# Index loads of two tiles each, fewer waits on TensorE and ScalarE, and four store buffers, in the edge loops of a graph network on one Trainium2 core

## The reference, cut to what matters

```
for s in range(S):                      # S = 2
    ce = concatenate([e, n[senders], n[receivers]], axis=-1)
    e = e + _ln(_mlp(ce, edge_blk_w0[s], ...), ...)
    agg = segment_sum(e, receivers, num_segments=num_nodes)
    cn = concatenate([n, agg], axis=-1)
    n = n + _ln(_mlp(cn, node_blk_w0[s], ...), ...)
```

## Time and profile before

| what | us |
|---|---|
| median of 3 runs (23509.02 to 23590.83) | 23560.08 |
| profiled execution, its own time | 23779.25 |
| its span, first to last instruction | 23777.4 |
| busy: PE / PEld / DVE / ACT / POOL | 12398.6 / 9600.5 / 7767.6 / 2986.5 / 12971.1 |
| mean granted TensorE clock | 0.627 |

### The profile page before, as it was taken

The page is one execution under the profiler, slowest core; times in us unless marked ns, Lnnn a source line. Parts: engine busy times, 40 slices in busy tenths (PEclk is TensorE's granted clock), DMA queues, the critical chain, the costliest instruction groups (busy, mean ns, idle before and its releaser), DMA issues. The chain is left out here.

```text
span 23777.4 us, 256036 instructions
## 1 busy us (share of the span) xinstructions
PE 12398.6 (52%) x61970; PEld 9600.5 (40%) x61970; DVE 7767.6 (33%) x22504; ACT 2986.5 (13%) x5247; POOL 12971.1 (55%) x13518
## 2 busy tenths in 40 slices
PE   0555565554232322325555656655556666666665
PEld 0444444443222222223444444444434444544454
DVE  2333333333111111112334434333333344343342
ACT  0222222221000000001111111111111111111111
POOL 2556565655666666662555555455435555555552
PEclk9566555565555555555667666666666666666675
DMA  1122222221000000001333333333323333333330
GB/s 50 52 54 56 54 55 55 55 55 47 12 11 11 11 11 11 11 11 22 99 102 107 107 102 104 103 105 104 103 60 94 100 98 99 99 99 98 99 101 14
DMA packets 2031268, 1570.78 MB, mean 66 GB/s; under 512 B 1340117, under 2 KB 1497177, under 8 KB 2029449
## 3 DMA queue, kind: packets, MB, share of 16 engines
q10 hardware_dynamic: 932082, 898.84, 11.7%
q0 software_dynamic: 446304, 295.04, 8.6%
q1 hardware_dynamic: 652511, 373.44, 5.7%
HBM read 961.50 MB, written 604.22 MB: 66 GB/s over the span
## 5 line engine op out<-in xcount | busy, mean ns | idle before, releaser
L720 POOL DMA_INDIRECT s_gt<-ta_d,s_ix x6448 | 6187.6, 960 | 5660.7 <-DMA s_ix<-in_src_s 2441.5
L863 PE MATMUL psw<-g_R,g_P 128*128 128x80 f32 (+1 forms) x12896 | 2673.2, 372 | 4261.8 <-ACT g_sg L793 3414.1
L863 PEld LDWEIGHTS psw<-g_R,g_P 128*128 128x128 f32 x12896 | 2568.8, 305 | 4795.9 <-issue 3827.8
L720 POOL DMA_INDIRECT g_gt<-xs_d,g_ix x3224 | 3048.8, 946 | 2077.7 <-DVE g_R L749 1106.8
L720 POOL DMA_INDIRECT g_gt<-ys_d,g_ix x3224 | 3049.7, 946 | 1798.9 <-issue 990.0
L608 DVE TENSOR_TENSOR g_P<-ps,dlT 128x1024 f32<-128x1024 f32 x806 | 985.3, 1222 | 5610.4 <-remote 4927.6
L863 PEld LDWEIGHTS psw<-s_R,s_P 128*128 128x128 f32 x12896 | 1908.9, 222 | 1705.1 <-issue 1702.8
L863 PE MATMUL psw<-s_R,s_P 128*128 128x64 f32 x12896 | 1877.4, 298 | 1057.3 <-issue 1020.0
L831 PE MATMUL ps<-e_w,s_hT 128*128 128x128 f32 x6448 | 1342.6, 375 | 1956.5 <-ACT s_hT L788 1679.1
L848 PE MATMUL ps<-s_Pt,s_Bw 128*64 128x128 f32 x12896 | 1535.7, 370 | 1009.8 <-issue 1008.2
L831 PEld LDWEIGHTS ps<-e_w,s_hT 128*128 128x128 f32 x6448 | 1181.8, 274 | 2084.2 <-ACT s_hT L788 1346.1
(11 more groups left out here) (289 smaller groups left out, 12961.8 us busy)
## 6 DMA issues: line engine op xcount, KB each, us to landing
s_dl<-dl_d SPq DMA_DIRECT2D x404, 512.0 KB
seg_d<-s_sg ACTq DMA_DIRECT2D x806, 256.0 KB
seg_d<-g_sg ACTq DMA_DIRECT2D x403, 320.0 KB
z_d<-g_rT ACTq DMA_DIRECT2D x403, 256.0 KB
s_z<-z_d ACTq DMA_DIRECT2D x403, 256.0 KB, 3.0
s_Bw<-tb_d ACTq DMA_DIRECT2D x3224, 32.0 KB
s_Bw<-tb_d SPq DMA_DIRECT2D x3224, 32.0 KB
s_gt<-ta_d,s_ix POOLq DMA_INDIRECT x6448
```

What stands on the lines that cost most here:

```text
L720: eng.indirect_dma_start(out=gt[k][:, s, :], out_offset=None, in_=table[:, :], in_offset=bass.IndirectOffsetOnAxis(ap=ix[h][:, r * G + s:r ...
L863: last = eng.matmul(psw[:, SP_ * t:SP_ * t + FS], P[k][:, s, :], R[k][:, s, :], start=True, stop=True)
```

## The change

It does five things, all in `edge_loop`.

1. `ix` gets four buffers of two tiles instead of two buffers of four. SP loads the indices of tiles j+2 and j+3 at every even j. In place of the four waits on landed gathers there is one, for `used` of tile j-5: `p_pre` in s0 and s1, `v_msg` in g1 and g2. At even j this also takes the place of the wait (for `p_pre` of tile j-6) ahead of SP's windows. In the program text the load now stands behind that of `dl` and, in g1, behind that of `z`.
2. `sg` and `rT` get four buffers; their writers wait for the store of four tiles ago.
3. PE loses waits: on the previous layer norm and silu, on landed gathers, windows and `z` (in s0, s1), on `v_p`. Those on landed data move to DVE, ahead of `Pt` of the same tile. In g1 PE waits for ACT's `zr` once, ahead of the segment sum instead of ahead of the transposes.
4. ACT loses its waits on `v_ln`, on `p_x`, and those ahead of its windows, and in s1 ahead of `z`.
5. In g1 and s0 DVE waits for `p_rt` ahead of `P` in place of `p_seg` there and `p_rt` ahead of `R`.

```
-s_ix, s_g, s_z, s_so, s_ro, s_dl ... (("ix", 2), ("g", 8), ("z", 8), ("so", 2), ("ro", 2), ("dl", 2))
+s_ix, s_g, s_z, s_so, s_ro, s_dl ... (("ix", 4), ("g", 8), ("z", 8), ("so", 4), ("ro", 4), ("dl", 2))
-ix = many("ix", [128, 4 * G], I32)
+ix = many("ix", [128, 2 * G], I32, n=4)
-sg = many("sg", [128, G * FS])
+sg = many("sg", [128, G * FS], n=4)
+used = p_pre if expand else v_msg
-    rT = many("rT", [128, 512])
+    rT = many("rT", [128, 512], n=4)
 def windows(eng, which, j, b, first):
-    done(eng, p_pre, j, L_BW + 4)
-    settle(eng, s_m[0])
...
 # SP
-def indices(q, i, b):
-    h = ((b + 2) // 4) % 2
-    for r in range(4):
-        landed(eng, s_g, G, i, b, 6 - r)
-        settle(eng, s_m[0])
-    eng.dma_start(ix[h][:, :], a["src_s"][bass.ds(q, 1), :, :]...).then_inc(s_ix[h].sem, 16)
...
-    if b % 4 == 2 and (not isinstance(j, int) or j + 2 < NIST):
-        indices(i * 2 + (b + 2) // 4, i, b)
     if stage(j, 0) and expand and b % 2 == 0:      # dl, unchanged
...
+    more = b % 2 == 0 and (not isinstance(j, int) or j + 2 < NIST)
+    if more or stage(j, L_BW) and expand:
+        done(eng, used, j, L_BW + (3 if more else 4))
+        settle(eng, s_m[0])
+    if more:
+        h = (b + 2) // 2 % 4
+        eng.dma_start(ix[h][:, :], a["src_s"][bass.ds(i * 4 + (b + 2) // 2, 1), :, :]...).then_inc(s_ix[h].sem, 16)
 # DVE
-    landed(eng, s_ro, 1, i, b, L_SUM + 2)
+    landed(eng, s_ro, 1, i, b, L_SUM + 4)
...
     done(eng, p_pre, j, L_PT + 2)
+    landed(eng, s_g, G, i, b, L_PT)
+    landed(eng, s_bw, G, i, b, L_PT)
+    landed(eng, s_zt, 1, i, b, L_PT)
...
-    done(eng, p_seg, j, L_LN + 2)
+    done(eng, p_rt if zout is not None else p_seg, j, L_LN + 2)
...
 # ACT
     done(eng, p_x, j, L_LN)
-    done(eng, v_ln, j, L_LN + 2)
...
     done(eng, p_pre, j, L_PRE)
-    done(eng, p_x, j, L_PRE + 2)
...
-    landed(eng, s_so, 1, i, b, L_SEG + 2)
+    landed(eng, s_so, 1, i, b, L_SEG + 4)
...
 # PE
     done(eng, a_h, j, L_LN)
-    done(eng, v_ln, j, L_LN + 2)
...
-    done(eng, a_h, j, L_PRE + 2)
     if expand:
-        landed(eng, s_g, G, i, b, L_PRE)
+        done(eng, v_pt, j, L_PRE)
...
-        landed(eng, s_bw, G, i, b, L_PRE)
-        done(eng, v_pt, j, L_PRE)
...
-    landed(eng, s_zt, 1, i, b, L_PRE)
+    if attr:
+        landed(eng, s_zt, 1, i, b, L_PRE)
...
-    done(eng, v_p, j, L_SEG)
-    if mlp:
-        done(eng, v_ln, j, L_SEG)
-    if ew2 is not None:
-        done(eng, v_msg, j, L_SEG)
-    done(eng, a_seg, j, L_SEG + 1)
+    if attr:
+        done(eng, a_zr, j, L_SEG)
+    else:
+        done(eng, v_ln if mlp else v_msg, j, L_SEG)
+        done(eng, a_seg, j, L_SEG + 1)
...
-    else:
-        done(eng, a_rt, j, L_SEG + 1)
-    if attr:
-        done(eng, a_zr, j, L_SEG)
```

More of the change, by code:

```diff
@@ L620, in build @@
         s_ix, s_g, s_z, s_so, s_ro, s_dl = [[mark(f"e_{n}{b}") for b in range(m)]
-                                            for n, m in (("ix", 2), ("g", 8), ("z", 8), ("so", 2), ("ro", 2), ("dl", 2))]
+                                            for n, m in (("ix", 4), ("g", 8), ("z", 8), ("so", 4), ("ro", 4), ("dl", 2))]
         def edge_loop(tag, FG, table, seg_d, mlp=None, attr=False, expand=False, zsrc=None, zw=None, zout=None, ew2=None):
@@ L675, in load_z @@
                         done(eng, v_sum, j, L_Z + DZ)
-                    else:
+                        settle(eng, s_m[0])
+                    elif attr:
                         done(eng, p_pre, j, L_Z + DZ)
-                    settle(eng, s_m[0])
+                        settle(eng, s_m[0])
                     src = a["attr_t"] if attr else zsrc
@@ L703, in step @@
                             load_z(eng, j, b)
+                        more = b % 2 == 0 and (not isinstance(j, int) or j + 2 < NIST)
+                        if more or stage(j, L_BW) and expand:
+                            done(eng, used, j, L_BW + (3 if more else 4))
+                            settle(eng, s_m[0])
+                        if more:
+                            h = (b + 2) // 2 % 4
+                            eng.dma_start(ix[h][:, :], a["src_s"][bass.ds(i * 4 + (b + 2) // 2, 1), :, :].rearrange("o p s -> p (o s)")
+                                          ).then_inc(s_ix[h].sem, 16)
                         if stage(j, L_BW) and expand:
@@ L710, in step @@
                         if stage(j, L_GA):
-                            k, r, h = (b - L_GA) % 8, (b - L_GA) % 4, (b - L_GA) // 4 % 2
+                            k, r, h = (b - L_GA) % 8, (b - L_GA) % 2, (b - L_GA) // 2 % 4
                             if r == 0 or isinstance(j, int):
@@ L759, in step @@
                                 eng.drain()
-                                if zout is not None:
-                                    done(eng, p_rt, j, L_LN + 2)
                                 eng.tensor_tensor(R[k][:, :, 0:64], ps[2 + k][:, :].rearrange("p (s f) -> p s f", s=G),
@@ L797, in step @@
                                 done(eng, p_rt, j, L_SEG)
-                                landed(eng, s_ro, 1, i, b, L_SEG + 2)
+                                landed(eng, s_ro, 1, i, b, L_SEG + 4)
                                 eng.activation(rT[k][:, :], ps[5][:, :], ACT.Copy, scale=gct[0][:, 0:1]).then_inc(a_rt.sem, 1)
@@ L804, in step @@
                         if stage(j, L_ST):
-                            k = (b - L_ST) % 2
+                            k = (b - L_ST) % 4
                             done(eng, a_seg, j, L_ST)
@@ L809, in step @@
                         if stage(j, L_DONE) and zout is not None:
-                            k = (b - L_DONE) % 2
+                            k = (b - L_DONE) % 4
                             if summed:
@@ L818, in act @@
                     drive(eng, step, L_DONE)
-                    for k in range(2):
-                        eng.wait_ge(*s_so[k](16 * turns(k, 2)))
+                    for k in range(4):
+                        eng.wait_ge(*s_so[k](16 * turns(k, 4)))
                         if zout is not None:
-                            eng.wait_ge(*s_ro[k](16 * turns(k, 2)))
+                            eng.wait_ge(*s_ro[k](16 * turns(k, 4)))
                 def pe(eng):
@@ L890, in edge_loop @@
                     s_z[k].passed(16 * turns(k, DZ))
+                for k in range(4):
+                    s_ix[k].passed(16 * ((NIT // 2 + 1 - k + 3) // 4))
+                    s_so[k].passed(16 * turns(k, 4))
+                    if zout is not None:
+                        s_ro[k].passed(16 * turns(k, 4))
                 for k in range(2):
-                    s_ix[k].passed(16 * ((NIT // 4 + 1 - k + 1) // 2))
-                    s_so[k].passed(16 * turns(k, 2))
-                    if zout is not None:
-                        s_ro[k].passed(16 * turns(k, 2))
                     if expand:
```

9 lines of the change are left out of this document (3 added, 6 removed).

## The result

The changed kernel takes 25,883 us (median of 4 runs, 25,798 to 25,936) against 23,555 us before: a ratio of 1.099, with an interval of 1.095 to 1.102. Its profiled execution has a span of 25883.4 us, 2,106 us more than that of before. The numbers can't be read without one more fact: the experiments ran on several chips, and there were two kinds of chip. On the one kind the kernel before takes 23,530 to 23,716 us, as in the profile ahead of the prediction; on the other it takes 18,390 to 18,433 us. I call them **A** and **B**. The time of every experiment is compared only with that of the kernel before on its own chip. The result above is from a chip of kind A.

A forecast was written before the change was run, and what follows sets the result against it. Bound: a cycle in which the other engines learn late of each other's work while POOL gathers and catch up when it stops. Terms 840 + 150 - 450 - 100 + 140 = +580 gave 24,140 us against 23,560; range 22,700 to 25,200.

The forecast's parts named there:

- two slower cases: The forecast of slower by a few per cent (0.40) and pairs locking (0.09), together 0.49.
- What bounds the kernel: All loops: while POOL gathers, other engines learn late of each other's work; they catch up when POOL stops.
- (a): Index loads of two tiles, all loops: load latency partly exposed after the release, +840 us, ends 0 and 1690.
- (b): s0 and s1: even tiles wait for t-7's projection, one tile less lead, +150 us, ends 0 and 3230.
- (c): Four store buffers: DVE's 3081.6 us wait for the store in s0 goes, two thirds of 677 gained, -450 us.
- (d): Waits left out on PE, ACT and SP: most idle time only changes its name, -100 us.
- (e): DVE waits for landed windows ahead of Pt: costs only where SP issues its half slowly, +140 us.
- (f): g1: segment sum behind zr, P behind the transposes; covered by POOL's gather time, 0, else 490 us.
- The locked rival: Loads wait until POOL stops, so every pair is one turn: about +2100 us, 25,700 us, chance 0.09.
- Signs to look for: Profile after: g1's gathers wait for g_ix, predicted us per tile by loop, rT's store wait gone, small s_Bw wait.

The follow-up runs named there:

- e3: Kernel before with only the new index loads (two tiles, four buffers, behind use of tile t-7): 25,986 us, 1.094, kind A.
- h1: Kernel before with two-tile index loads in four buffers behind landed gathers of t-8 and t-7: 24,115 us against 23,672, 1.017, kind A.
- h2: Kernel before with POOL's even tiles waiting for use of t-7 instead of t-8, loads as before: 24,452 us against 23,530, 1.039, kind A.
- e4: Kernel before with only four store buffers added: 23,178 us, 0.977, kind A.
- e2: Changed kernel with the old index loads (four tiles, two buffers, behind landed gathers): 23,861 us, 1.006 of before, kind A.
- e1: Changed kernel with the landed waits back on PE instead of on DVE ahead of Pt: 25,145 us, 1.060 of before, kind A.
- e6: Changed kernel with old index loads and landed waits back on PE: 18,455 us, 1.002 of before, kind B.
- f4: The changed kernel itself, run on a chip of kind B: 18,350 us against 18,433 before, 0.996.

## Why the prediction was wrong

The direction was right, with a chance of 0.49 for its two slower cases; the size was not. Forecast +580, measured +2,328, outside the range.

- **What bounds the kernel**: right for this chip. All of the loss is POOL's idle time, and the others do catch up in POOL's stops. What the argument left unused is its own first finding: if the others work mostly in and around stops, then an edit that changes how many tiles POOL gathers per turn changes more than a latency. I priced latencies and one shift, and no term of the sum had the length of a turn in it.
- **(a) loads, +840, and (b) lead, +150**: together +990, measured +2,271 (e3), the larger of the two misses. The two taken singly are +443 (h1, within (a)'s ends, half of what I took) and +922 (h2, six times what (b) took).

  The first step that failed is in (b): "in a cycle where the others set the pace, a fixed shift is paid once and not per turn". h2 is exactly that shift, and s1 pays it with 98 stops fewer. The second is in (a): "the load is issued about when POOL runs dry", behind use of t-7. In g1 and g2 it does stand behind use of t-7; in s0 and s1 it stands behind `dl`, and so behind `Pt` of t-5, and it goes out 18.4 and 19.4 us (medians of s0 and s1) after POOL has run dry. The part on the change says that the load moved behind that of `dl`; no term priced it.

  The sum of the two also lacked the 906 us that neither h1 nor h2 has.

  The Trainium skill, "SBUF — State Buffer", section "The DMA setup-cost knee", has a fixed cost of about 2 us per transfer, from which I had an estimate of 808 us if every load were exposed. h1, with the same number of loads guarded by landings, measured 443 us and nothing in g1 and g2, so there most are hidden; e3 measured 2,271, more than all 404 loads at 3.34 us each (1,349).
- **(c) stores, -450**: -538 (e4), all in s0. Right; the difference between s0 and s1 was a good price for it, but that two thirds of it would come was a guess.
- **(d) and (e), -100 and +140**: together +683 with the old loads (e2 against e4). With the new ones (e) is some +900 (the changed kernel against e1, on two chips), six times what I took, and (d) -303 if the parts add. (e) was said to be wrong if `Pt` became DVE's largest wait. In s0 and s1 it did: 4374.8 us for the windows. The failed step is "it costs only where SP is slow with its half (16.53 us)". SP's half was not what `Pt` waited for, but ACT's, which stands behind the silu of the tile two before: DVE stood 22.20 us, 13 of them after SP's last window was issued, with the layer norm of another tile queued behind. The sign was in the row that I read: in the kernel before `Pt` started ahead of ACT's last window (23.06 against 23.19), and it did so in 84% of the tiles of s1. PE has no layer norm behind its own wait. Without (e) and the new loads (d) ran only on a chip of kind B (e6, with the store buffers: +0.2%).
- **(f)** g1's new chain, 0: e2's g1 is 5111 against e4's 5063, so +48 us, with what (d) does there, in one execution each.
- **The locked rival** gave 25,700 and a chance of 0.09. It came closest, partly by luck: it had g2 at 14.4 us per tile (12.17 measured) and nothing in s0 (+469). And what it locked was not pairs: 83 of the 115 turns in s1 are of four tiles.
- **Signs to look for**: g1 waiting for `g_ix`, 13.5 and 12.3 us per tile in g1 and g2 (13.81 and 12.17 measured), the store's wait gone: seen. s1 at 13.9 and s0 at 14.6 (16.11 and 16.22): here the sum broke. The line of `Pt` was to wait for `s_Bw` by a few hundred us, and it was 4374.8.

## What to carry to other kernels

A wait that implies another is not equal to it: the count that comes later (use in place of landing) gives away lead, and so does a wait that moves to an engine with other work queued behind it. Price both by the engine that stands behind the wait, not by the instruction saved. What a load waits for is the latest of all waits ahead of it in its queue, not the one written beside it: when a load moves behind another, ask what that other waits for. If a profile shows one engine stopping in a regular beat while the others catch up, count the tiles between its stops, and ask of each edit whether it makes them more; here this went with the loss in s0 and s1, without being shown to be its cause. And compare a kernel with its predecessor on the same chip, then on another: here the same edit was 9.9% slower on one and 0.4% faster on another.

## What was not expected of the hardware

The two kinds of chip. The same instructions of the changed kernel, SP's and ACT's for the windows, seen by line: first on the chip of the result (kind A), then in f4 (kind B). The columns are duration in ns, least, median and largest.

```profile
L668 ACTq MOVE s_Bw<-tb_d x3224: 3/29/1397, 11824.7 to 25264.4; - x190
...
L668 SPq ALU_OP  x3224: 2/37/1399, 11826.5 to 25254.7; - x190
```

```profile
L668 ACTq MOVE s_Bw<-tb_d x3224: 29/29/38, 9380.7 to 17814.7; - x190
...
L668 SPq ALU_OP  x3224: 32/37/54, 9382.5 to 17802.0; - x190
```

The medians agree. On kind B no register move of ACT for the windows lasts over 38 ns; on kind A some last up to 1397 ns. They fall for the most part in the stretches where POOL gathers: of SP's register instructions in s0 and s1 of the changed kernel, 2039 of the 3248 begun while POOL gathered lasted over 0.1 us, and 386 of the 4747 begun in a stop; of ACT's, 126 of 2938 and 9 of 7545. In f4 none did. A gather lasts POOL the same on both (943 and 948 ns in g1), and `Pt` lasts DVE 760 ns on both. So on kind A the instruction streams of SP and ACT are held up while POOL issues indirect DMAs, and on kind B they are not. That the late counts of PE and DVE are the same thing is likely, since they too are missing on kind B, but it was not traced. Nothing in the runs shows what differs between the chips; that was not tried. The experiments met three chips of kind A and four of kind B (the chip of the result, of kind A, may be one of the three), and each held its kind through all runs on it (10 and 25 runs of the kernel before on two of them, within 0.5%).
